# TensorE signals twice instead of four times per group: octet counts and early sums are waited for through the signal of the projected rows

## The chip, the cores and the metric

The kernel runs on one core of one Trainium2 chip. The time is the device time of one execution in microseconds (us). The kernel before takes 3303.69 us (median of 3 runs, 3300.82 to 3312.31). Differences of about 0.3% are the least that such runs tell from no change.

## The reference

Two graph layers over 12,500 nodes of 64 features and 212,500 edges sorted by destination (padded here to 208 groups of 1024 edges, 8 edges on each of 128 partitions):

```python
def _L0_gnn_ref(x, i, j, rbf, Wf1, bf1, Wf2, bf2, Wl, bl, gamma, beta):
    Wxh = x @ Wl.T + bl
    h = jax.nn.silu(rbf @ Wf1.T + bf1)
    f_ij = h @ Wf2.T + bf2
    msg = f_ij * Wxh[j]
    agg = jax.ops.segment_sum(msg, i, num_segments=x.shape[0])
    y = x + agg
    ...
def _L1_gnn_ref(x, edge_index, edge_weight, W1, b1, W2, b2):
    msg = x[src] * edge_weight[:, None]
    agg = jax.ops.segment_sum(msg, dst, num_segments=x.shape[0])
    h = jax.nn.relu((agg + x) @ W1 + b1)
    return h @ W2 + b2
...
edge_index = jnp.stack([src, dst])
x = _layernorm(x + _L0_gnn_ref(x, src, dst, edge_attr_64, edge_weight, ...), axis=-1)
x = _layernorm(x + _L1_gnn_ref(x, edge_index, edge_weight, ...), axis=-1)
```

The call is `_L0_gnn_ref(x, src, dst, edge_attr_64, ...)`: the first layer gathers at `dst` (sorted, so a group of edges needs only a short window of node rows) and sums at `src` (unsorted).

## The kernel before, in words

The change lies in `sorted_messages`, the first large stage. It walks over the 208 groups in 52 passes of S = 4 groups. For each group it computes the messages of 1024 edges, splits them into three bf16 parts, finds for each edge its rank within the block of 128 nodes it is summed into, and writes each edge's row to that block's region in memory (`region_rows`). There are 98 blocks. From pass 27 on the finished first rows of a block are already summed ("early sums"), one block per group, while later messages are still written: 7 tiles of 128 rows per block at first, 9 from pass 33, 10 from pass 39, 12 from pass 45 (`EARLY`), so groups 108, 132, 156 and 180 open these parts, and group 207 is the last.

Each engine has its own queue in program order, and engines meet only through semaphores. Per group (i, j), with the line numbers of the kernel before:

- TensorE (PE): `blocks` makes running counts by block from one-hot matrices (L1096, L1099, into `counts`) and the octet counts (L1102, L1104, into `ps_pairs`), and signals `rk` at L1104. `nodes` projects the node rows of the window onto the edges, six matmuls into `ps_x` (L1114), and signals `xw`. Then the two filter matmuls of the following groups (L1121, L1091), `back` (four transposes of the product, L1128), and `early_sums` (three matmuls a tile, L1138, signal `e_mm`).
- VectorE (DVE), in `steady`: `early_total` (L1252, adds an early sum to x), `products` (L1228), the one-hots and the window of the next group (L1179, L1181, L1188), `rest_part` (L1233), `earlier` of the next group (L1194 to L1199, where L1197 writes into a row buffer and first waits until the scatter of four groups before has landed, `sc[j]`), `low_part` (L1237, completes the rows of this group), `positions` of the next group (L1204 to L1221, where L1208 reads `counts`), and `early_onehot` (L1244).
- ScalarE (ACT): activations and the copies of the parts (L1026, L1030, L1035, L1039, L1049, L1051).
- GpSimd (POOL): `scatter`, eight indirect DMAs per group (their issue is L1332). A group's scatter waits for its positions (L1221) and for its last part (`lw`, signalled by L1237, which is the later one).
- SyncE (SP): loads of edge features, node windows and the finished rows of blocks (L974, L984, L986, L989).

`count_of(i, j, back)` is the number of groups done up to group (i, j), less `back`; each semaphore is seeded with S. After the last group, POOL waits for all scatters and the stage that sums the remaining rows begins (L1527 and on).

Of the kernel before, what the change touches and what calls it, by code (L numbers as in the profile page):

```python
# [78 lines left out]
def program(nc, n_nodes, n_edges, x, x_t, src, dst, dst_next, dst_rows, firsts, group_dst, ew, rbf, w, out, wxh_rows, x1_rows, sorted_rows, q_block_row,  # L79
# [13 lines left out]
    with ctx:  # L93
# [183 lines left out]
        def count_of(i, j, back=0):  # L277


            return i * S + (S + 1 + j - back)  # L280
# [579 lines left out]
        def sorted_messages():  # L860
# [31 lines left out]
            e_ld = [own(f"e_ld_{u}") for u in range(RING)]  # L892
            e_kc, e_oh, e_mm = (own(f"e_{k}") for k in ("kc", "oh", "mm"))
            at = width + T * D
# [52 lines left out]
            with nc.Block(no_gpsimd_drain=True) as block:  # L947
# [18 lines left out]
                def _(e):  # L966
                    r = rbf.rearrange("(b p) n -> b p n", p=P)
                    q = rel_rows.rearrange("(b t) p -> b (t p)", t=BATCH * T)
                    def early_load(n):
                        if n.opens:  # L970
                            for j in range(S):
                                e.wait_ge(sc[j], (early_starts[n.stage] - BEHIND) * (16 * T) + 16 * T)
                        e.wait_ge(e_mm, n.number + 1)
                        e.dma_start(early_rows[n.slot][:, 0:n.tiles * RW // 2],  # L974
                                    region_rows[bass.ds(n.number * STRIDE, n.tiles * P), :].rearrange("(p t) w -> p (t w)", p=P)
                                    ).then_inc(e_ld[n.slot], 16)
# [106 lines left out]
                def _(e):  # L1083
                    seed(e, rk, xw, bk, e_mm)
                    empty = block_iota[:, :, :].rearrange("p n t -> p (n t)")[:, 0:PAIRS]
# [7 lines left out]
                    def blocks(i, j):  # L1093
                        e.wait_ge(ww, count_of(i, j, 1))
                        for t in range(0, T, TQ):
                            e.matmul(counts, not_tri[:, :], onehot_n((j + 1) % 2)[:, :, t:t + TQ], start=(t == 0), stop=False)  # L1096
                        e.wait_ge(oh, count_of(i, j))
                        for t in range(0, T, TQ):
                            e.matmul(counts, tri[:, :], onehot_n(j % 2)[:, :, t:t + TQ], start=False, stop=(t + TQ == T))  # L1099
                        e.wait_ge(ob, count_of(i, j))  # L1100
                        for t in range(0, T, TQ):
                            e.matmul(ps_pairs[0:NB, 0:NB * TQ], block_of_octet[j % 2][:, 0, :], onehot_n(j % 2)[:, :, t:t + TQ],  # L1102
                                     start=False, stop=False)
                        last = e.matmul(ps_pairs[0:NB, NB * TQ:PAIRS], block_of_octet[j % 2][:, 1, :], moved[:, tiles(i, j)],  # L1104
                                        start=False, stop=False)
                        last.then_inc(rk, 1)

# [23 lines left out]
                    def early_sums(i, j, n):  # L1131
                        e.wait_ge(e_oh, n.number + 1)
                        e.wait_ge(m, count_of(i, j))
                        rows = early_rows[n.slot].bitcast(BF16).rearrange("p (t w) -> p t w", w=RW)
                        place = early_places[n.slot % 2][:, 0:P * n.tiles].rearrange("p (n t) -> p n t", t=n.tiles)
                        for t in range(n.tiles):
                            for c in range(PARTS):
                                last = e.matmul(early_sum, place[:, :, t], rows[:, t, c * D:(c + 1) * D],  # L1138
                                                start=(t == 0 and c == 0), stop=(t == n.tiles - 1 and c == PARTS - 1))
                        last.then_inc(e_mm, 1)  # L1140

# [31 lines left out]
                def _(e):  # L1173
                    seed(e, oh, ob, wi, c1, c2, c3, bs, ba, ww, pr, pr2, po, m, r1, lw, me)

                    def block_onehot(i, j):
                        e.wait_ge(rk, count_of(i, j, 1))
                        e.wait_ge(ww, count_of(i, j, 2))
# [22 lines left out]
                    def positions(i, j):  # L1201
# [3 lines left out]
                        e.wait_ge(ww, count_of(i, j, 1))  # L1205
                        e.wait_ge(rk, count_of(i, j))
                        e.wait_ge(ba, count_of(i, j, 1))
# [32 lines left out]
                    def early_onehot(n):  # L1240
                        e.wait_ge(e_kc, n.number + 1)
                        e.wait_ge(e_mm, n.number + S - 1)
                        place = early_places[n.slot % 2][:, 0:P * n.tiles].rearrange("p (n t) -> p n t", t=n.tiles)
                        e.tensor_tensor(place, early_keys[:, 0:1, bass.ds(n.at, n.tiles)].broadcast_to([P, P, n.tiles]),  # L1244
                                        iota_rep[:, :, 0:n.tiles], ALU.is_equal).then_inc(e_oh, 1)

                    def early_total(n):
                        e.wait_ge(e_mm, n.number + S + 1)
                        if isinstance(n.number, int) and n.number == 0:
# [5 lines left out]
                    def steady(i, j, now=None, before=None):  # L1255
                        if before and before.exists:
                            early_total(before)
                        products(i, j)
# [40 lines left out]
                    for j in range(S - 1):  # L1299
                        steady(passes - 1, j, unit(passes - 1, j, K, False), unit(passes - 1, j, K, False, 2))  # L1300
                    early_total(unit(passes - 1, S - 1, K, False, 2))
                    products(passes - 1, S - 1)
                    rest_part(passes - 1, S - 1)
                    low_part(passes - 1, S - 1)

                    e.wait_ge(rk, S * passes + S + 1)
                    step(e.tensor_reduce(run[:, :], counts.rearrange("p (n t) -> p n t", t=TQ), AX.X, ALU.add))
# [1267 lines left out]
```

## Time and profile before

| | |
|---|---|
| median of 3 runs | 3303.69 us |
| the profiled execution, its own time | 3301.68 us |
| its span in the profile | 3299.7 us |
| mean granted TensorE clock | 0.80 of full |
| busy share of the span | DVE 78%, POOL 71%, PE 62%, ACT 30% |
| message stage: first and last indirect DMA start on POOL | 129.7 us, 2258.9 us |

A busy share is an average over stages with different limits, so what bounds the message stage is read from that stretch alone. A duration is the time an engine held an instruction; "idle" is the time the engine stood before it, with what released it ("issue" where the profile names no releaser). The granted clock of TensorE is in tenths of its full 2.4 GHz; in the message stage it moves between its two levels, 1.0 (2.4 GHz) and 0.5 (1.2 GHz).

### The profile page before, as it was taken

What the parts mean: (1) busy time and instruction counts of PE and PEld (TensorE: products, weight loads), DVE (VectorE), ACT (ScalarE), POOL (GpSimd) and SP (SyncE); (2) the same over time, 40 slices, a digit from 0 to 9 for tenths busy, and PEclk for the clock granted to TensorE, in tenths of its full rate; (3) what the DMA queues carried; (4) which work ended last, traced back from release to release, by engine and by line L of the source; (5) the groups of instructions that cost most, each with busy time, mean ns of one, the idle gap of its engine ahead of it and who ended that gap; (6) DMA issues with size and microseconds to landing.
All of it is one profiled execution on the core that took longest, in us unless ns stands there. A gap on an engine that the chain in (4) does not pass through costs nothing. (4 is left out here: it accounts for less than half of the span.)

```text
span 3299.7 us, 57203 instructions
## 1 busy us (share of the span) xinstructions
PE 2051.3 (62%) x18002; PEld 1373.3 (42%) x18002; DVE 2563.1 (78%) x4987; ACT 1001.9 (30%) x2288; POOL 2335.0 (71%) x2177
## 2 busy tenths in 40 slices
PE   2655565656555556666676666663783666658886
PEld 2222222222222233333444444443773655547775
DVE  6877777777777777778787787774875999978887
ACT  3222222222222222222222222221676666641001
POOL 0677777777777777777777777774234888868775
PEclk8888878787887788888888888886755677769999
DMA  7743445333333334444444445434654999989997
GB/s 199 196 124 124 124 124 150 95 95 94 94 95 93 95 116 127 127 135 138 134 142 144 143 151 153 147 98 139 194 166 152 354 363 358 357 324 405 395 392 286
DMA packets 261217, 605.85 MB, mean 184 GB/s; under 512 B 112847, under 2 KB 130127, under 8 KB 248375
## 3 DMA queue, kind: packets, MB, share of 16 engines
q1 hardware_dynamic: 186330, 385.45, 38.1%
q0 software_dynamic: 67488, 210.15, 17.3%
q10 hardware_dynamic: 7205, 7.74, 0.9%
q8 instruction: 113, 1.85, 0.2%
q14 instruction: 81, 0.66, 0.1%
HBM read 403.92 MB, written 199.25 MB: 183 GB/s over the span
## 5 line engine op out<-in xcount | busy, mean ns | idle before, releaser
L1332 POOL DMA_INDIRECT region_rows<-x_space,pos x1664 | 1657.4, 996 | 531.4 <-issue 504.2
L1128 PE MATMUL ps_cnt<-ident,work 128*128 128x128 f32 x832 | 178.2, 353 | 760.2 <-DVE work L1228 760.2
L1035 ACT CAST x_space<-ps_cnt 128x512 bf16<-128x512 f32 x208 | 121.7, 585 | 1461.9 <-PE ps_cnt L1128 1461.9
L1128 PEld LDWEIGHTS ps_cnt<-ident,work 128*128 128x128 f32 x832 | 116.6, 176 | 931.2 <-issue 931.2
L1217 DVE TENSOR_REDUCE rank<-work 128x8 f32<-128x784 f32 x208 | 323.4, 1555 | 21.8 <-DVE work L1213 0.5
L1121 PE MATMUL ps_fx<-work,w_wf 128*128 128x512 f32 x416 | 253.6, 694 | 67.6 <-ACT work L1026 66.7
L1233 DVE TENSOR_TENSOR work<-ps_cnt,x_space 128x512 f32<-128x512 f32 x208 | 143.8, 691 | 124.8 <-ACT x_space L1035 124.8
L1091 PE MATMUL ps_th<-x_space,w_wf 128*128 128x512 f32 x416 | 220.4, 613 | 9.4 <-DMA x_space<-rbf 9.4
L1114 PE MATMUL ps_fx<-work,x_space 128*64 128x512 bf16 x1248 | 225.3, 478 | 0.0
L1213 DVE TENSOR_TENSOR work<-onehot,ps_rank 128x784 f32<-128x784 bf16 x208 | 201.9, 971 | 7.2
L1197 DVE COPY x_space<-edges_space 128x16 f32 (+1 forms) x208 | 39.8, 191 | 212.5 <-DMA region_rows<-x_space,pos 212.0
L2051 DVE TENSOR_TENSOR x_space<-x_space,iota_rep 128x3328 bf16<-128x3328 bf16 x98 | 195.9, 1999 | 3.6 <-PE ps_th L2090 0.2
L1871 PE MATMUL ps_th<-x_space,tmp_space 128*128 128x64 bf16 x1764 | 127.9, 222 | 102.8 <-DVE tmp_space L1834 102.8
L1039 ACT CAST x_space<-work 128x512 bf16<-128x512 f32 x208 | 128.6, 618 | 174.3 <-DVE work L1233 174.3
L1871 PE MATMUL ps_fx<-x_space,tmp_space 128*128 128x64 bf16 x1764 | 128.0, 222 | 72.1 <-DVE tmp_space L1834 72.1
L1834 DVE TENSOR_SCALAR tmp_space<-tmp_space,scalars 128x1152 bf16<-128x1152 bf16 x196 | 161.4, 824 | 10.5 <-DMA tmp_space<-key_rows 10.5
L1237 DVE TENSOR_TENSOR x_space<-work,x_space 128x512 bf16<-128x512 f32 x208 | 143.3, 689 | 31.8 <-ACT x_space L1039 30.7
L1908 POOL TENSOR_TENSOR x_space<-tmp_space,x_space 128x576 f32<-128x576 f32 x80 | 137.8, 1723 | 37.0 <-ACT x_space L1887 37.0
L1871 PEld LDWEIGHTS ps_th<-x_space,tmp_space 128*128 128x128 bf16 x1764 | 114.1, 116 | 116.5 <-DVE tmp_space L1834 116.5
L1096 PE MATMUL ps_rank<-onehot,not_tri 128*128 128x392 bf16 x416 | 156.2, 471 | 0.0
L1208 DVE TENSOR_REDUCE run<-ps_rank 128x98 f32<-128x392 f32 x208 | 116.3, 559 | 48.2 <-issue 43.8
L1099 PE MATMUL ps_rank<-onehot,tri 128*128 128x392 bf16 x416 | 152.0, 459 | 0.0
(276 smaller groups left out, 5322.1 us busy)
## 6 DMA issues: line engine op xcount, KB each, us to landing
tmp_space<-key_rows SPq DMA_DIRECT2D x98, 576.0 KB, 7.7
x_space<-rbf SPq DMA_DIRECT2D x104, 512.0 KB, 3.8
tmp_space<-rel_rows SPq DMA_DIRECT2D x104, 512.0 KB, 4.1
region_rows<-x_space,pos POOLq DMA_INDIRECT x1664
tmp_space<-region_rows SPq DMA_DIRECT2D x48, 441.0 KB, 4.1
tmp_space<-region_rows SPq DMA_DIRECT2D x25, 588.0 KB, 5.1
region_rows<-x_space SPq DMA_DIRECT2D x12, 1176.0 KB, 7.2
tmp_space<-region_rows SPq DMA_DIRECT2D x25, 539.0 KB, 4.5
```

Of the source, the lines that this page charges most:

```text
L1091: return e.matmul(ps_hid[j % 2], wts["wf1"][:, :], inputs_t[j], start=True, stop=True)
L1096: e.matmul(counts, not_tri[:, :], onehot_n((j + 1) % 2)[:, :, t:t + TQ], start=(t == 0), stop=False)
L1099: e.matmul(counts, tri[:, :], onehot_n(j % 2)[:, :, t:t + TQ], start=False, stop=(t + TQ == T))
L1114: last = e.matmul(ps_x[h * D:(h + 1) * D, :], near[j][:, c * D:(c + 1) * D], window_half(j, h), start=(c == 0), stop=(c == PARTS - 1))
L1121: return e.matmul(ps_f[:, :], wts["wf2"][:, :], hid[j % 2][:, :], start=True, stop=True)
L1128: last = e.transpose(ps_cnt[:, t * P:(t + 1) * P], product[:, t * P:(t + 1) * P], ident[:, :])
L1213: e.tensor_tensor(masked_n, onehot_n(j % 2), base_ps.unsqueeze(2).broadcast_to([P, NB, T]), ALU.mult).then_inc(ww, 1)
L1217: e.tensor_reduce(rank8[:, :], masked_n.rearrange("p n t -> p t n"), AX.X, ALU.add).then_inc(pr, 1)
L1332: e.indirect_dma_start(out=region_rows, out_offset=bass.IndirectOffsetOnAxis(ap=pos[j][:, t:t + 1], axis=0), in_=rows_f[j][:, t, :], in_of ...
L1834: e.tensor_scalar(which[n % 2], key_bc[b % KB][:, (n % 2) * U * P:(n % 2 + 1) * U * P], node_1, None, ALU.is_equal).then_inc(oh, 1)
L1871: last = e.matmul(ps_rows[n % 2][:, t, :], which[n % 2][:, t * P:(t + 1) * P], x1_part(n // 2, c), start=(c == 0), stop=(c == PARTS - 1))
L2051: e.tensor_tensor(places[c % 2], place[c % 2].unsqueeze(1).broadcast_to([P, P, RUN]), iota_rep[:, :, :], ALU.is_equal).then_inc(oh, 1)
```

## The change

The signals of `blocks` (`rk`, one a group) and of `early_sums` (`e_mm`, one a block) are taken away. Who waited for them waits for `xw`, which PE signals at the end of `nodes`, or for nothing where an earlier wait on `xw` on the same queue already covers it. `rk` is kept for the one last matmul after the loop. No matmul, DMA or vector instruction is added, removed or moved.

```diff
-                        e.wait_ge(e_mm, n.number + 1)
                         e.dma_start(early_rows[n.slot][:, 0:n.tiles * RW // 2],
...
-                    seed(e, rk, xw, bk, e_mm)
+                    seed(e, xw, bk)
...
-                        last = e.matmul(ps_pairs[0:NB, NB * TQ:PAIRS], block_of_octet[j % 2][:, 1, :], moved[:, tiles(i, j)],
-                                        start=False, stop=False)
-                        last.then_inc(rk, 1)
+                        e.matmul(ps_pairs[0:NB, NB * TQ:PAIRS], block_of_octet[j % 2][:, 1, :], moved[:, tiles(i, j)],
+                                 start=False, stop=False)
...
-                                last = e.matmul(early_sum, place[:, :, t], rows[:, t, c * D:(c + 1) * D],
-                                                start=(t == 0 and c == 0), stop=(t == n.tiles - 1 and c == PARTS - 1))
-                        last.then_inc(e_mm, 1)
+                                e.matmul(early_sum, place[:, :, t], rows[:, t, c * D:(c + 1) * D],
+                                         start=(t == 0 and c == 0), stop=(t == n.tiles - 1 and c == PARTS - 1))
...
                     def block_onehot(i, j):
-                        e.wait_ge(rk, count_of(i, j, 1))
+                        e.wait_ge(xw, count_of(i, j, 1))
...
                         e.wait_ge(ww, count_of(i, j, 1))
-                        e.wait_ge(rk, count_of(i, j))
+                        e.wait_ge(xw, count_of(i, j))
                         e.wait_ge(ba, count_of(i, j, 1))
                         e.tensor_reduce(run[:, :], counts.rearrange("p (n t) -> p n t", t=TQ), AX.X, ALU.add).then_inc(bs, 1)
...
                     def early_onehot(n):
                         e.wait_ge(e_kc, n.number + 1)
-                        e.wait_ge(e_mm, n.number + S - 1)
...
-                    def early_total(n):
-                        e.wait_ge(e_mm, n.number + S + 1)
+                    def early_total(n, i, j):
+                        e.wait_ge(xw, count_of(i, j))
...
-                    e.wait_ge(rk, S * passes + S + 1)
+                    e.wait_ge(rk, 1)
```

Below is VectorE's queue in a pass with early sums of 10 tiles, from the end of one group's positions to the product of the next group, before the change. In brackets stand the semaphores that an instruction waits for: stage0_15 is `rk`, stage0_12 is `xw`, stage0_40 is `e_mm`, stage0_38 is `e_kc`, stage0_20 is `ww`.

```order
L1204 TENSOR_REDUCE same<-same 128x8 [waits stage0_17,stage0_23]
L1208 TENSOR_REDUCE run<-ps_rank 128x98 [waits stage0_31,stage0_15,stage0_20]
L1211 TENSOR_TENSOR ps_rank<-ps_rank,run 128x98 [waits stage0_19,stage0_21]
L1221 SCALAR_TENSOR_TENSOR pos<-rank,edges_space 128x8 [waits stage0_22]
L1244 TENSOR_TENSOR x_space<-tmp_space,iota_rep 128x1280 [waits stage0_40,stage0_38]
L1252 TENSOR_TENSOR agg<-ps_agg,x_space 128x64 [waits stage0_40]
L1228 TENSOR_TENSOR work<-ps_fx,work 128x512 [waits stage0_12,stage0_10,stage0_11]
```

And the same place after it, where the lines have moved up by three or four:

```order
L1201 TENSOR_REDUCE same<-same 128x8 [waits stage0_17,stage0_23]
L1205 TENSOR_REDUCE run<-ps_rank 128x98 [waits stage0_31,stage0_12,stage0_20]
L1208 TENSOR_TENSOR ps_rank<-ps_rank,run 128x98 [waits stage0_19,stage0_21]
L1218 SCALAR_TENSOR_TENSOR pos<-rank,edges_space 128x8 [waits stage0_22]
L1240 TENSOR_TENSOR x_space<-tmp_space,iota_rep 128x1280 [waits stage0_38]
L1248 TENSOR_TENSOR agg<-ps_agg,x_space 128x64 [waits stage0_12]
L1225 TENSOR_TENSOR work<-ps_fx,work 128x512 [waits stage0_12,stage0_10,stage0_11]
```

The instructions stand in the same order; the reduction of the counts now waits for `xw` instead of `rk`, the early one-hot has one wait less, and the early total waits for `xw`.

## Rows read from the trace of the kernel before

**Rows 1.** The page, part 1: busy us, share of the span, instructions.
```profile
PE 2051.3 (62%) x18002; PEld 1373.3 (42%) x18002; DVE 2563.1 (78%) x4987; ACT 1001.9 (30%) x2288; POOL 2335.0 (71%) x2177
```

**Rows 2.** Busy by stretch: width, busy (instructions) per engine, PEclk, DMA share, GB/s.
```profile
130.00:1186.00 1056.00, 597.69 (x2163) 275.90 (x2162) 758.18 (x1654) 243.73 (x412) 807.41 (x816) 0.81 0.37 110
1433.00:1683.00 250.00, 168.61 (x1140) 99.23 (x1140) 199.70 (x436) 62.05 (x144) 191.47 (x193) 0.82 0.46 137
1683.00:1933.00 250.00, 169.77 (x1218) 103.33 (x1218) 200.16 (x438) 62.22 (x144) 191.16 (x194) 0.83 0.48 143
1933.00:2226.50 293.50, 199.71 (x1563) 127.78 (x1563) 232.85 (x500) 72.13 (x165) 225.69 (x223) 0.82 0.45 135
```

**Rows 3.** L1332, 130 to 2260 us: durations ns min/median/max, starts; idle by releaser.
```profile
L1332 POOL DMA_INDIRECT region_rows<-x_space,pos x1638: 965/969/1590, 129.7 to 2258.9; - x182
  issue: 496.9, 1630
```

**Rows 4.** L1197 in four stretches: durations, starts; then idle before it (us, times).
```profile
L1197 DVE COPY x_space<-edges_space x103: 167/176/372, 136.5 to 1184.8; 128x16 f32 x103
  DMA region_rows<-x_space,pos: 168.3, 62
...
L1197 DVE COPY x_space<-edges_space x24: 166/170/310, 1437.1 to 1676.3; 128x16 f32 x20, 128x16 f32<-128x16 f32 x4
  DMA region_rows<-x_space,pos: 9.9, 9
...
L1197 DVE COPY x_space<-edges_space x24: 166/170/377, 1686.6 to 1926.4; 128x16 f32 x20, 128x16 f32<-128x16 f32 x4
  DMA region_rows<-x_space,pos: 6.6, 4
...
L1197 DVE COPY x_space<-edges_space x28: 167/169/346, 1936.6 to 2224.2; 128x16 f32 x21, 128x16 f32<-128x16 f32 x7
```

**Rows 5.** Timeline at 2001 us, clock at its full level: start, us, instruction.
```profile
2000.87 0.17 PE L1104 MATMUL ps_agg<-edges_space,block_of_octet 128*98 x1
2000.96 0.84 PE L1114 MATMUL ps_fx<-work,x_space 128*64 128x512 bf16 x6
2001.13 0.57 DVE L1208 TENSOR_REDUCE run<-ps_rank 128x98 f32<-128x392 f32 x1 [0.37 <-issue]
```

**Rows 6.** Timeline at 1438 us, clock at its lower level.
```profile
1438.49 0.21 PE L1104 MATMUL ps_agg<-edges_space,block_of_octet 128*98 128x8 bf16 x1
1438.62 1.50 PE L1114 MATMUL ps_fx<-work,x_space 128*64 128x512 bf16 x6
```

**Rows 7.** L1208 in the last three stretches: durations, starts; idle before it.
```profile
L1208 DVE TENSOR_REDUCE run<-ps_rank x24: 554/566/568, 1438.8 to 1678.6; 128x98 f32<-128x392 f32 x24
  issue: 10.2, 17
...
L1208 DVE TENSOR_REDUCE run<-ps_rank x24: 548/567/568, 1688.8 to 1928.6; 128x98 f32<-128x392 f32 x24
  issue: 10.5, 21
...
L1208 DVE TENSOR_REDUCE run<-ps_rank x28: 565/567/568, 1938.8 to 2225.7; 128x98 f32<-128x392 f32 x28
  issue: 21.9, 27
```

**Rows 8.** L1114 on PE, stretches from 1433 and from 1933: durations, starts.
```profile
L1114 PE MATMUL ps_fx<-work,x_space x144: 378/403/636, 1438.6 to 1679.2; 128*64 128x512 bf16 x144
...
L1114 PE MATMUL ps_fx<-work,x_space x168: 378/379/637, 1938.7 to 2226.0; 128*64 128x512 bf16 x168
```

**Rows 9.** Timeline at the stage's end: last L1237, first DMA of group 207, next stage.
```profile
2234.13 0.69 DVE L1237 TENSOR_TENSOR x_space<-work,x_space 128x512 bf16<-128x512 f32 x1 [0.68 <-ACT x_space L1039]
...
2249.98 0.96 POOL L1332 DMA_INDIRECT region_rows<-x_space,pos  x1 [0.30 <-issue]
...
2262.26 1.28 ACT L1527 ACT_TABLE_LOAD   x1 [28.16 <-PEq L947]
```

More of the change, by code:

```diff
@@ L892, in sorted_messages @@
             e_ld = [own(f"e_ld_{u}") for u in range(RING)]
-            e_kc, e_oh, e_mm = (own(f"e_{k}") for k in ("kc", "oh", "mm"))
+            e_kc, e_oh = (own(f"e_{k}") for k in ("kc", "oh"))
             at = width + T * D
@@ L1256, in steady @@
                         if before and before.exists:
-                            early_total(before)
+                            early_total(before, i, j)
                         products(i, j)
@@ L1300, in _ @@
                         steady(passes - 1, j, unit(passes - 1, j, K, False), unit(passes - 1, j, K, False, 2))
-                    early_total(unit(passes - 1, S - 1, K, False, 2))
+                    early_total(unit(passes - 1, S - 1, K, False, 2), passes - 1, S - 1)
                     products(passes - 1, S - 1)
```

## The prediction

> **What bounds the kernel now.** I first read the page's busy shares. They name VectorE (78%) ahead of GpSimd (71%) [rows 1], which is an average over all stages. The change acts only in the message stage, so I read that stage alone. Its indirect DMAs start from 129.7 to 2258.9 us, and 1630 of the 1638 waited for nothing but their own issue: 496.9 / 1630 = 0.30 us each, behind 0.97 us of work [rows 3]. GpSimd is therefore a solid chain of 1.27 us steps, eight a group, a little over 10.2 us a group (191.47 us busy in 250 is the same 0.97 in 1.27) [rows 2]. It is never starved after the start. The message stage ends when GpSimd ends, and the next stage starts 2 to 3 us later [rows 9].
>
> VectorE runs ahead of GpSimd. How far, and with what slack, decides this change. Two readings give it:
>
> - The brake. L1197 may not fill a row buffer before the scatter of four groups ago has landed. Where VectorE stands there, it has time to spare. Up to 1186 us it stood 168.3 us in 103 groups, 1.6 us a group. From 1433 it stood 9.9 us in 24 groups, from 1683 6.6 us in 24, and from 1933 not at all in 28 [rows 4]. So VectorE, which also does early one-hots and totals there, has spare time at first and none at the end.
> - The lead. For the last group, L1237 ends at 2234.13 + 0.69 = 2234.82, and GpSimd starts that group's scatter at 2249.98 [rows 9]. The rows lie finished for 15.2 us. This is the stock that can be eaten before GpSimd waits.
>
> Then I looked at what VectorE waits for in the late part. L1208, which reads the running counts, stood 10.2, 10.5 and 21.9 us in the last three stretches, before 17 of 24, 21 of 24 and 27 of 28 groups [rows 7]. The profile calls this "issue", but the timeline shows whose it is: at 2001 us the octet matmul L1104 ends at 2000.87 + 0.17 = 2001.04 and L1208 starts at 2001.13, after 0.37 us idle [rows 5]. It is the wait on `rk`. So in the late part VectorE is bound through TensorE: early sums, then the counts, then L1208.
>
> **The change, part by part.**
>
> *L1208 waits for `xw` instead of `rk`.* It now starts after the six matmuls of L1114 too, which stand right behind L1104. At the full clock they end at 2000.96 + 0.84 = 2001.80, 0.76 us behind L1104 [rows 5]. At the lower clock they end at 1438.62 + 1.50 = 1440.12, 1.42 us behind its 1438.70 [rows 6]. In a group where L1208 already waited, all of this is added. The instructions behind it on VectorE (positions, early one-hot, total, the next product) are late by as much, and so are the transposes and early sums on TensorE, which wait for that product, and ScalarE's copies. They all hang on VectorE's chain and shift with it, so nothing makes the time good except the stand at L1197.
>
> I moved the start of each L1208 to the end of that group's last L1114 plus the 0.09 us seen between L1104 and L1208. The added delay sums to 19.9 us in the 24 groups from 1433 (0.83 each), 20.1 us in the next 24 (0.84) and 22.3 us in the last 28 (0.80). These means lie near the full-clock 0.76, as they should: the median L1114 takes 379 to 403 ns, the longest 636 [rows 8], so most groups see the full clock and some the lower. Sum: 62.3 us.
>
> *What is absorbed.* Before 1433 all of it: the delay is under 1.5 us in any group, adds to 34.6 us over 131 groups, and the stand at L1197 is many times that (168.3 us up to 1186 alone) [rows 4]. From 1433, following the groups in order and letting each stand at L1197 swallow the lateness collected so far, 8.0 of the 9.9 us are used, and 6.3 of the 6.6. VectorE then is late by 62.3 - 8.0 - 6.3 = 48.0 us at the last group.
>
> *What is left on the end.* The lead of 15.2 us covers the first part; it is used up near group 170 (about 1835 us), and from there GpSimd waits once a group for L1237. 48.0 - 15.2 = 32.8 us remain. The stages behind start when the last scatter is done, so they shift by this whole.
>
> *The other waits.* `block_onehot` waits for `xw` of a group whose product has just waited for the same count: nothing. `early_total` waits for `xw` of the group whose product stands right behind it, and that count has been waited for already in the positions before: nothing new. `early_onehot` and SyncE's loads of block rows lose a wait that an earlier `xw` wait covers. The transfers are issued when the queue comes to them, as before. What a dropped wait frees on VectorE no row shows. I bound it by the 0.09 us from the end of L1104 to the start of L1208 [rows 5], over 76 groups 7 us, and from below by 0; I take 0, since the remaining wait of the same instruction stays.
>
> *Taking the signals off TensorE.* The octet matmul with its signal ends at 2001.04, and L1114 has started at 2000.96, before it [rows 5]. The signal holds nothing up, so I take 0. The most it could hide is the 0.09 us between the starts of the two matmuls (2000.87 and 2000.96); for two signals over 76 groups that is 14 us, which I keep for the range. The Trainium skill, "TensorE: Matmul & The Clock Gate", section "The cost: per-tile semaphore tail", says that increments on completion serialize at about 26 ns each; it speaks for this change. By it, two signals less in each of 76 groups would give back an estimated 4 us, and the sum would be 29 instead of 33. The trace does not show such a tail behind L1104.
>
> *The sum.* The profiled execution took 3301.7 us, and 3301.7 + 32.8 = 3334.5. The median of the runs lies 2.0 us above that execution, so I forecast 3336, 1.0% slower. Bounds of this mechanism: with the 7 us of the dropped wait and the 14 us of the signals it is 33 - 21 = 12 (3316); another 0.09 us a group, should `xw` come through later than `rk`, gives 33 + 7 = 40 (3344).
>
> **The rivals.**
>
> - *The lead swallows it: no change.* VectorE works 15 us ahead and stands at L1197 for 16.5 us from 1433 on [rows 4, 9], so up to 15.2 + 14.3 = 29.5 us over 76 groups cost nothing. This decides when the real delay is under 29.5 / 76 = 0.39 us a group, half of what the rows show. It could be so if the modelled ends of matmuls stood too late, or if VectorE came to L1208 later for another reason. The start of L1208 0.09 us behind the modelled end of L1104 [rows 5] speaks against it. Time: 3304. Chance 0.12.
> - *Faster: collisions ease.* GpSimd's issue takes 965 ns at best but up to 1590 [rows 3], perhaps where it meets VectorE's wide operations; the mean up to 1186 us is 807.41 / 816 = 989 ns [rows 2]. If VectorE's shifted position took such meetings away, the gain is at most 0.024 us x 1638 = 39 us. It decides only if GpSimd stays the bound, so the lead has to hold as well, and VectorE still runs as many wide operations per group. A third of it gives 3304 - 13 = 3291. Chance 0.03.
> - *Slower still: TensorE's clock.* TensorE now idles 0.8 us longer in each late group. The granted clock is 0.82 to 0.83 there [rows 2]. If it fell to the lower level throughout, L1114 would add 1.42 instead of 0.82 a group, another 46 us over 76, besides longer early sums. A part of this, 15 to 30 us, gives 3350 to 3366. Against it: up to 1186 us TensorE is busy for only 57% of the time, and its clock is 0.81 all the same, as against 68% and 0.82 at the end [rows 2]. So I give it 0.10.
> - The mechanism as summed: 0.75.
>
> **How the numbers follow.** The likeliest case alone gives 3316 to 3344. For 8 in 10 I reach down into the lead rival (partly absorbed) and up to the lower end of the clock rival: 3311 to 3351. A measurement here tells about 0.3% (10 us) from no change. Faster: 0.03. Same: the lead rival, 0.12. Slower: 0.85.
>
> **What would show it.** In the profile after: the idle before the counts' reduction (now L1205) rises from 21.9 us to about 44 in the last 28 groups. GpSimd waits for L1234 (was L1237) at about one DMA in eight from some 1840 us on, some 33 us in all. The stand at L1194 (was L1197) in the stretches from 1433 nearly vanishes. The stretch up to 1186 and all after the message stage keep their length. The prediction is wrong if GpSimd is still never starved at 2200 us, if the reduction starts before the last L1112 (was L1114) ends, or if the added time lies behind the message stage.

## The result and the profile after

The changed kernel takes 3369.72 us (median of 4 runs, 3366.35 to 3373.26), the kernel before on the same chip 3302.26 us. The ratio is 1.020, interval 1.0175 to 1.0221: slower by 67 us, where 33 us were forecast, and outside the stated range (3311 to 3351).

The page of the changed kernel, part 1, in the columns of [rows 1]. VectorE, ScalarE and GpSimd are busy for at most 6 us more. TensorE is busy for 37.2 us more with the same 18002 matmuls, 15 us of it before 1189 us, where nothing is lost (next table). The span is longer by 68.7 us.

```profile
span 3368.4 us, 57021 instructions
...
PE 2088.5 (62%) x18002; PEld 1397.5 (41%) x18002; DVE 2569.0 (76%) x4987; ACT 1001.9 (30%) x2288; POOL 2338.0 (69%) x2177
```

Busy time by stretch, as in [rows 2]: the first is the same stretch without early sums, the others are groups 132 to 155, 156 to 179 and 180 to 207.

```profile
133.00:1189.00 1056.00, 612.74 (x2165) 283.26 (x2163) 760.85 (x1655) 243.63 (x413) 807.84 (x815) 0.81 0.37 110
1440.00:1711.00 271.00, 171.42 (x1142) 101.93 (x1143) 201.71 (x439) 62.06 (x144) 205.94 (x204) 0.80 0.44 129
1711.00:1985.00 274.00, 173.97 (x1228) 106.06 (x1227) 201.35 (x439) 62.28 (x145) 191.65 (x193) 0.80 0.44 131
1985.00:2308.50 323.50, 208.25 (x1557) 131.01 (x1555) 230.93 (x495) 72.05 (x165) 226.36 (x220) 0.79 0.40 121
```

Up to 1189 us GpSimd issues 815 DMAs where it issued 816: nothing is lost there. The three stretches of early sums take 271, 274 and 324 us where they took 250, 250 and 294, and their granted clock is 0.80, 0.80, 0.79 instead of 0.82, 0.83, 0.82.

The counts' reduction (now L1205) in the same stretches, as in [rows 7]:

```profile
L1205 DVE TENSOR_REDUCE run<-ps_rank x24: 565/567/568, 1445.3 to 1704.7; 128x98 f32<-128x392 f32 x24
  issue: 34.1, 24
...
L1205 DVE TENSOR_REDUCE run<-ps_rank x24: 565/567/567, 1716.8 to 1977.9; 128x98 f32<-128x392 f32 x24
  issue: 36.6, 24
...
L1205 DVE TENSOR_REDUCE run<-ps_rank x28: 565/566/567, 1990.1 to 2307.0; 128x98 f32<-128x392 f32 x28
  issue: 51.7, 28
```

It now stands in every group, for 34.1, 36.6 and 51.7 us against 10.2, 10.5 and 21.9. The period is (1704.7 - 1445.3) / 23 = 11.28 us a group, then 11.35 and 11.74, against 10.43, 10.43 and 10.63. The stand at the row buffer (now L1194) has no row in any of the three.

A group of the last stretch in the timeline: the reduction starts 0.11 us behind the end of L1112 (2011.28 + 0.84 = 2012.12), not behind L1103, and GpSimd waits for the last part of the rows.

```profile
2010.20 0.69 DVE L1234 TENSOR_TENSOR x_space<-work,x_space 128x512 bf16<-128x512 f32 x1 [0.29 <-ACT x_space L1038]
...
2011.18 0.17 PE L1103 MATMUL ps_agg<-edges_space,block_of_octet 128*98 128x8 bf16 x1
...
2011.28 0.84 PE L1112 MATMUL ps_fx<-work,x_space 128*64 128x512 bf16 x6
...
2011.74 0.97 POOL L1328 DMA_INDIRECT region_rows<-x_space,pos  x1 [0.79 <-DVE x_space L1234]
...
2012.23 0.57 DVE L1205 TENSOR_REDUCE run<-ps_rank 128x98 f32<-128x392 f32 x1 [1.21 <-issue]
```

GpSimd over the whole stage, as in [rows 3]. It is starved 79 times, in the last third of the stage; the first time that it stands for more than 1 us is in group 153. (These waits include the 0.30 us that each issue costs anyway.)

```profile
L1328 POOL DMA_INDIRECT region_rows<-x_space,pos x1639: 963/969/1728, 130.1 to 2327.2; - x183
  issue: 487.3, 1560
  DVE x_space L1234: 61.8, 53
  DVE pos L1218: 7.9, 26
```

The end of the stage, as in [rows 9]: the last L1234 ends at 2315.83, and the first DMA of the last group starts at 2318.25. The lead has shrunk from 15.2 to 2.4 us. By the same reading, group by group, it is under 1.5 us for the first time in group 150, where the prediction had it used up near group 170.

```profile
2315.14 0.69 DVE L1234 TENSOR_TENSOR x_space<-work,x_space 128x512 bf16<-128x512 f32 x1 [0.68 <-ACT x_space L1038]
...
2318.25 0.97 POOL L1328 DMA_INDIRECT region_rows<-x_space,pos  x1 [0.30 <-issue]
...
2330.54 1.28 ACT L1523 ACT_TABLE_LOAD   x1 [15.44 <-PEq L947]
```

The balance closes. The last reduction of counts starts at 2307.0 instead of 2225.7, 81.3 us later; the lead gives back 15.2 - 2.4 = 12.8; and the last group's scatter starts 2318.25 - 2249.98 = 68.3 us later. The next stage begins 2330.54 - 2262.26 = 68.3 us later, and nothing is added behind it.

So place and chain are as forecast, and the loss is twice the forecast one. **Where the other half of the loss lies.** At group 107, before any early sum, the changed kernel's execution is already 3.1 us later. That leaves 78.2 us of lateness made in groups 108 to 207, where the prediction had 48.0. Going through the trace of before once more, row by row, with another rule for the stands at L1197 gives 64.5 (theory B below; 63.5 with the 0.09 us of the prediction between the rows' end and the reduction, 65.4 with the 0.11 us seen after). Some 3.3 us of it arise in groups 108 to 131, where the prediction had nothing; the reductions of groups 107 and 131 lie 3.2 us farther apart after than before.

That leaves 13.7 us. TensorE's way can be measured by itself: from the start of the product to the end of the projected rows took 5.94, 5.99 and 6.14 us on average in the three stretches before, and takes 6.03, 6.13 and 6.49 after; 24 x 0.09 + 24 x 0.14 + 28 x 0.35 = 15 us, with the granted clock down as above. The same sum is 17 us for e2 below, which has the same wait moved, and 3.5 us for e1, which is as fast as the kernel before, so it holds to a few us.

**Theory A** is the prediction's: lateness is swallowed by each stand at the row buffer. **Theory B**: the stand lies behind the product in VectorE's queue, and TensorE's way (transposes, early sums, counts, rows) starts at the product. The two run side by side. Where TensorE's way is the longer one, arriving late at the stand shortens only the shorter way, and nothing is given back. A stand gives back at most the time by which VectorE's own way is longer. B was made up after the result; the runs below test it.

### The profile page after: what moved, and what is told of

It is laid out like the page before. It is cut to its first block and busy times, and to the rows that moved or that the text cites. A ratio compares the mean times of both kernels' runs of the same rounds, so it can differ in the third digit from the quotient of the medians.

```text
span 3368.4 us, 57021 instructions
## 1 busy us (share of the span) xinstructions
PE 2088.5 (62%) x18002; PEld 1397.5 (41%) x18002; DVE 2569.0 (76%) x4987; ACT 1001.9 (30%) x2288; POOL 2338.0 (69%) x2177
## 3 DMA queue, kind: packets, MB, share of 16 engines
q1 hardware_dynamic: 186330, 385.45, 37.2%
## 5 line engine op out<-in xcount | busy, mean ns | idle before, releaser
L1126 PE MATMUL ps_cnt<-ident,work 128*128 128x128 f32 x832 | 191.6, 374 | 824.9 <-DVE work L1225 824.9
L1126 PEld LDWEIGHTS ps_cnt<-ident,work 128*128 128x128 f32 x832 | 124.8, 187 | 994.8 <-issue 994.8
L1205 DVE TENSOR_REDUCE run<-ps_rank 128x98 f32<-128x392 f32 x208 | 117.0, 562 | 160.1 <-issue 155.2
L1112 PE MATMUL ps_fx<-work,x_space 128*64 128x512 bf16 x1248 | 232.2, 490 | 0.0
L1234 DVE TENSOR_TENSOR x_space<-work,x_space 128x512 bf16<-128x512 f32 x208 | 143.4, 689 | 38.0 <-ACT x_space L1038 37.3
L1904 POOL TENSOR_TENSOR x_space<-tmp_space,x_space 128x576 f32<-128x576 f32 x80 | 138.0, 1725 | 37.2 <-ACT x_space L1883 37.2
L1194 DVE COPY x_space<-edges_space 128x16 f32 (+1 forms) x208 | 40.0, 192 | 158.8 <-DMA region_rows<-x_space,pos 158.5
```

The costliest lines, as they stand in the source:

```text
L1112: last = e.matmul(ps_x[h * D:(h + 1) * D, :], near[j][:, c * D:(c + 1) * D], window_half(j, h), start=(c == 0), stop=(c == PARTS - 1))
L1126: last = e.transpose(ps_cnt[:, t * P:(t + 1) * P], product[:, t * P:(t + 1) * P], ident[:, :])
```

## The experiments

**Which wait, and do signals cost?** The first gives the changed kernel its signal at the octet counts back; the second moves only one wait in the kernel before.

```diff
 # e1, against the changed kernel
-                        e.matmul(ps_pairs[0:NB, NB * TQ:PAIRS], block_of_octet[j % 2][:, 1, :], moved[:, tiles(i, j)],
+                        last = e.matmul(ps_pairs[0:NB, NB * TQ:PAIRS], block_of_octet[j % 2][:, 1, :], moved[:, tiles(i, j)],
...
+                        last.then_inc(rk, 1)
...
                     def positions(i, j):
-                        e.wait_ge(xw, count_of(i, j))
+                        e.wait_ge(rk, count_of(i, j))
...
 # e2, against the kernel before
                     def positions(i, j):
-                        e.wait_ge(rk, count_of(i, j))
+                        e.wait_ge(xw, count_of(i, j))
```

> The changed kernel with one signal given back: the octet matmul signals again, and only the reduction of the counts waits for it; the signal of the early sums stays away and every other wait stays on the projected rows. If the whole loss is the wait of the counts' reduction (theory A and B alike), this is the kernel before: 3302 us, ratio to before 0.998 to 1.002. If a part of the loss comes from the early totals, the early one-hots or SyncE's loads, now ordered through the projected rows, this part stays: with half of the loss 3335 us.

> The kernel before with one wait moved: the reduction of the counts waits for the projected rows; all four signals are still given and all other waits are as before. If the loss is that wait: 3370 us, ratio 1.020, within 5 us of the changed kernel. If signals on TensorE cost what the Trainium skill's figure gives (an estimated 4 to 5 us for two signals in each of some 76 to 98 groups), it is that much above the changed kernel, 3375. If the other waits carried a part, it is below 3360.

Measured: e1 3297.4 us against 3296.5, ratio 1.0007 (0.9994 to 1.0019). e2 3367.4 us, ratio 1.0225 (1.0199 to 1.0251). The one wait of the counts' reduction is the whole loss. The early totals, the one-hots and SyncE's loads on another signal are worth nothing (e1, to within 6 us). For the signals taken off TensorE the times are too coarse to settle 4 us: e2 gives them all and is as slow as the changed kernel, but each of the two ratios is known to some 8 us only. The traces settle it. In the groups from 108 on whose six row matmuls ran at 2.4 GHz, the first of them starts 97 ns (median) behind the start of the octet matmul, in the kernel before, in e1 and in e2, where that matmul signals, and in the changed kernel, where it does not. From the start of the last early sum to that of the next counts matmul the medians are 59 ns before, 60 in e2 and 59 after. A signal holds up nothing here. GpSimd's waits in e2:

```profile
L1332 POOL DMA_INDIRECT region_rows<-x_space,pos x1637: 963/969/1735, 130.0 to 2327.4; - x182
  issue: 490.9, 1571
  DVE x_space L1237: 55.8, 45
  DVE pos L1221: 6.4, 21
```

**The dose.** The changed kernel with two, or eight, instead of six matmuls ahead of the signal.

```diff
                     def nodes(i, j):
 # e3
-                            for c in range(PARTS):
-                                last = e.matmul(ps_x[h * D:(h + 1) * D, :], near[j][:, c * D:(c + 1) * D],
-                                                window_half(j, h), start=(c == 0), stop=(c == PARTS - 1))
+                            last = e.matmul(ps_x[h * D:(h + 1) * D, :], near[j][:, 0:D],
+                                            window_half(j, h), start=True, stop=True)
...
 # e4
-                            for c in range(PARTS):
+                            for n_, c in enumerate((0, 0, 1, 2)):
...
```

> The changed kernel with a smaller dose: the node rows are projected from the first of their three bf16 parts alone, so two matmuls stand between the octet counts and the signal instead of six, and the second and third part are left out of the result. The added delay per group falls from about 0.8 to about 0.3 us. Theory A, the bookkeeping of the prediction (each stand at the row buffer swallows the lateness collected so far): lateness at the last group 16 us, 2 us of it beyond the lead, time 3304. Theory B (a stand swallows nothing in a group where the way over TensorE is the longer one, since that way starts at the product, ahead of the stand): lateness 25 us, 11 us beyond the lead, time 3313.

> The changed kernel with a larger dose: the first part is added twice, eight matmuls instead of six ahead of the signal, so the projected rows are not those of the reference. Theory A: 50 us beyond the lead, time 3352. Theory B: 74 us beyond the lead from the row by row account alone, and with the 14 to 17 us that the changed kernel showed beyond that account (a longer way over TensorE at a lower granted clock, some us of the start) 3390 us.

Measured: e3 3309.4 us, ratio 1.0042 (1.0026 to 1.0057), 13 us over the kernel before; A had 2, B 11. e4 3391.0 us, ratio 1.0294 (1.0268 to 1.0320), 94 us; A had 50 (64 to 67 if it is given the 14 to 17 us of TensorE's longer way too), B 88 to 91 with them. The lateness made in groups 108 to 207, by the starts of the reduction in the traces, is 20 us in e3 (A 16, B 25) and 108 in e4 (A 65, B 89, both without TensorE's longer way, which from the product to the end of the octet counts alone is 14 us longer in e4 than before). The larger dose rules A out even with that share: 65 + 14 = 79 against 108. The smaller one does not decide: its time speaks for B, its lateness lies midway, and its profiled execution, at 3298.3 us, was the fastest of eight, 11 us under their median. No stand at the row buffer is left in groups 132 to 207 of either.

**TensorE's clock.** The changed kernel with 30 small matmuls a group more, in the gap ahead of the transposes.

```diff
                         if left > 2:
                             after(hidden, i, j, 2)
+                        for _ in range(30):
+                            e.matmul(ps_pairs[0:NB, PAIRS:512], tri[:, 0:NB], not_tri[:, 0:512 - PAIRS], start=False, stop=False)
                         back(i, j)
...
```

> The changed kernel with 30 small matmuls (112 columns each) more per group on TensorE, in the gap in which it waits for the product, into columns that nothing reads. If the way over TensorE is longer in the changed kernel because the longer gap costs granted clock, the share of the lower level falls, the last stretch's period goes from 11.75 to about 11.3 us a group, and the time is 3350 to 3356. If the granted clock has nothing to do with the gap, 3370. If the filling itself is too long for the gap (at the lower clock it may be), the transposes start late and the time is over 3375.

Measured: 3340.2 us, ratio 1.0117 (1.0091 to 1.0144), faster than the expectation had even for the case that the clock is the cause. By the ratios, useless matmuls take back (1.0198 - 1.0117) x 3302 = 27 us of the 67. From 1433 to 2250 us the profiles give, for the kernel before:

```profile
1433.00:2250.00 817.00, 540.15 (x3928) 331.54 (x3928) 639.48 (x1387) 197.60 (x455) 626.14 (x627) 0.82 0.45 135
```

for the changed kernel:

```profile
1433.00:2250.00 817.00, 521.86 (x3671) 318.36 (x3670) 596.77 (x1293) 186.19 (x431) 589.19 (x582) 0.80 0.44 132
```

and with the gap filled:

```profile
1433.00:2250.00 817.00, 618.36 (x6006) 431.56 (x6004) 618.24 (x1328) 191.05 (x443) 613.00 (x601) 0.87 0.45 135
```

The granted clock is the last but two: 0.82, 0.80, 0.87. With the wait moved, TensorE idles longer in each group and is granted less; kept busy in the idle time, it is granted more than in the kernel before. Time at the 1.2 GHz level from group 132 to 207 is 35%, 41% and 26%. From product to rows takes 5.68, 5.68 and 6.16 us in the three stretches with the gap filled, 28 us less in sum than in the changed kernel and 13 less than in the kernel before. So the 27 us gained lie on TensorE's way, and they are more than the 14 to 15 us of the change, since the fill also takes back some of what the lower level costs in the kernel before. The Trainium skill, "TensorE: Matmul & The Clock Gate", in its section "Why this matters for your kernels", advises against idle gaps between bursts of matmuls; the traces of this kernel on these chips agree.

The gap itself is TensorE's idle time ahead of the transposes, which wait for the product. One tile's instructions on PE, durations and starts, then the idle time before them, first in the changed kernel, then in the kernel before:

```profile
L1126 PE MATMUL ps_cnt<-ident,work x304: 272/421/448, 1440.8 to 2302.0; 128*128 128x128 f32 x152
...
  DVE work L1225: 316.1, 76
```

```profile
L1128 PE MATMUL ps_cnt<-ident,work x304: 272/303/448, 1434.5 to 2222.3; 128*128 128x128 f32 x152
...
  DVE work L1228: 259.0, 76
```

It is 316.1 / 76 = 4.2 us a group after and 259.0 / 76 = 3.4 before, and the median transpose takes 421 ns instead of 303.

**Early sums into the gap.** The sums moved ahead of the transposes (`early_sums` before `back`), the total behind `low_part` of the same group with a signal for TensorE.

> The changed kernel with two signals kept, but the early sums moved from behind the transposes to ahead of them, into the gap in which TensorE waits for the product; the early total moves on VectorE to behind the last part of the same group, one group sooner, and signals TensorE. The 2.3 us of sums leave the way from the product to the counts. Theory B: that way falls from 6.5 to about 4.2 us, VectorE's own work becomes the longer way (period under 10.2 us if it were free), the stands at the row buffer come back, GpSimd is never starved, time 3302 (ratio 0.998 to 1.003). If the moved wait on the projected rows costs by itself, wherever TensorE's work lies, it stays slower than 3330.

Measured: 3335.8 us, ratio 1.0094 (1.0078 to 1.0109). B missed it (3302). By its number the run falls to the other side of the expectation (over 3330), but not by its mechanism: the moved wait hardly acts here. The reduction of the counts stood for 5.1 us in all before 14 of 76 groups:

```profile
L1205 DVE TENSOR_REDUCE run<-ps_rank x76: 550/556/568, 1441.6 to 2273.2; 128x98 f32<-128x392 f32 x76
  issue: 5.1, 14
```

The timeline shows that the sums are not in the gap:

```profile
2104.80 0.96 DVE L1240 TENSOR_TENSOR x_space<-tmp_space,iota_rep 128x1536 bf16<-128x1536 bf16 x1 [0.20 <-issue]
2105.68 0.68 DVE L1225 TENSOR_TENSOR work<-ps_fx,work 128x512 f32<-128x512 f32 x1
2105.89 2.40 PE L1136 MATMUL ps_agg<-tmp_space,x_space 128*128 128x64 bf16 x36 [3.10 <-DVE x_space L1240]
...
2108.11 1.09 PE L1126 MATMUL ps_cnt<-ident,work 128*128 128x128 f32 x4
```

They wait for the early one-hot (L1240), which VectorE writes last before the product (L1225). So they begin only as the gap ends, and the transposes, which ScalarE and VectorE wait for, start 2.43 us behind the product here and 2.03 on average, against 0.83 in the kernel before and in the changed one. VectorE stands 149.4 us in 77 groups for ScalarE's copy of the transposed product, against 43.9 in 76 before. So the sums, started this late, hold up VectorE's way instead. e6 says nothing on whether the moved wait can be hidden.

**Where in the group does a delay count?** One vector operation more per group in the kernel before (half of the ranks' product, into a buffer that is overwritten), ahead of the counts' reduction (e7) or behind it (e8).

```diff
+                        e.tensor_tensor(masked_n[:, 0:NB // 2, :], onehot_n(j % 2)[:, 0:NB // 2, :],
+                                        block_iota[:, 0:NB // 2, :], ALU.mult).then_inc(xt, 1)
```

> The kernel before with one vector operation of about 0.5 us more per group, placed ahead of the reduction of the counts, that is beside TensorE's way from the product to the counts. Theory B: it is hidden behind that way where TensorE is the longer one and swallowed by the stands elsewhere; row by row it leaves 3 us of lateness at the last group and nothing beyond the lead: 3302, ratio 0.999 to 1.002. If any 0.5 us in VectorE's group counted in the late part, 76 x 0.5 = 38 us less the stands and the lead: 3310 to 3320.

> The kernel before with the same vector operation just behind the reduction of the counts, in series with TensorE's way. Theory B: it counts in full where TensorE is the longer way and the stands give nothing back there: lateness 33 us, 18 us beyond the lead, time 3320 (ratio 1.004 to 1.007), and some us more if the granted clock falls as in the changed kernel. By the bookkeeping of the prediction (38 us less 14 us of stands less 15 us of lead) 3311.

Measured: e7 3317.5 us, ratio 1.0036 (1.0022 to 1.0050); e8 3313.6 us, ratio 1.0031 (1.0020 to 1.0042). The times don't tell the theories apart: GpSimd is hardly starved in either. This is e7:

```profile
L1337 POOL DMA_INDIRECT region_rows<-x_space,pos x1641: 965/969/1725, 129.3 to 2279.8; - x183
  issue: 497.8, 1633
  DVE x_space L1242: 1.8, 6
```

The leads do say something: 16.4 us at the last group in e7 and 7.5 in e8 (15.2 before). From group 131 to 207 VectorE falls back by 8.0 us in e7, in step with GpSimd, and by 16.3 in e8. Ahead of the reduction the 0.56 us mostly hid; behind it they ate half of the lead. There they lengthened the stretch from reduction to product by only 0.26 us on average, since they partly filled a semaphore gap, which is why e8 was smaller than planned. Of 76 x 0.26 = 20 us, 16 are left at the end, though L1197 had 16.5 us of stands to give: that fits B better than A. The time lost in both came from elsewhere, for which the last section has a partial answer.

**Runs that settle nothing.** On three other chips the kernel before took 4076, 4083 and 4086 us instead of 3300, so the runs made on them can't be set beside the others. The granted clock is 0.70 to 0.74 in them where it was 0.81 in the stretch up to 1186 us [rows 2]; this row is of e9:

```profile
133.00:1189.00 1056.00, 529.71 (x1714) 238.66 (x1715) 681.53 (x1481) 194.16 (x328) 656.08 (x654) 0.71 0.30 90
```

GpSimd is starved there from the first groups on, so the question of the stage's lead doesn't arise. The extra time lies in the message stage alone: from the last reduction of counts to the end takes 1054 us in e9 and 1074 in the kernel before. e9 and e10 are e7 and e8 with the other half of the operation as well, e11 is the kernel before with the fill of e5, and e12 is e6 with sums and totals a group later. e13 to e18 are the same kernels again.

> The kernel before with two vector operations of 0.56 us more per group, ahead of the reduction of the counts. The single one ahead cost 11 us without ever starving GpSimd, whose mean step went from 996 to 1006 ns. Twice that is some 20 us. Beside it theory B (hidden beside TensorE's way, up to its length) gives 24 to 28 us of lateness and 8 to 12 us beyond the lead: 3322 to 3335. If the place in the group did not matter, it is as slow as the kernel with the two behind the reduction.

> The same two operations just behind the reduction of the counts. The single one of 0.56 us lengthened the stretch from the reduction to the next product by only 0.27 us, since it fills a semaphore gap; the second one counts in full, so 0.84 us a group in series. Theory B: lateness 60 us, 44 us beyond the lead, and with GpSimd's slower steps up to group 131 (some 12 us) 3350 to 3362. By the bookkeeping of the prediction 76 x 0.84 less 14 less 15 = 34, and 12: 3340 to 3348, and if the place did not matter the same as with the two ahead.

> The kernel before with the 30 small matmuls per group in TensorE's gap. The share of time at the lower clock falls as it did in the changed kernel (0.41 to 0.26 from group 132 on), but GpSimd is the bound all through the stage: 3302, ratio 0.998 to 1.002, with a larger lead at the last group (over 17 us instead of 15). If TensorE's clock bounds this kernel anywhere in the stage, it is faster by 5 us or more.

> The kernel with the sums in the gap, mended: in it the sums waited for the early one-hot, which VectorE writes last before the product, so they started only as the gap ended (the sums waited 3.1 to 3.4 us for L1240 in a group) and the transposes came behind them. Here the sums and the total of a block come one group later, when its one-hot has long been written, so they can fill the gap; SyncE's loads wait for the total instead. Still two signals from TensorE per group beside the transposes' and those of the filters. Theory B: the way from product to counts falls from 6.5 to about 4.2 us, stands at the row buffer come back, GpSimd is never starved: 3302, ratio 0.998 to 1.003. If the later signal costs whatever TensorE's order is, over 3330.

> The kernel with two vector operations ahead of the reduction of the counts, where the kernel before takes its usual 3300 us. Expected as for its first run: 3322 to 3335 by theory B.

> The kernel with two vector operations behind the reduction of the counts. Expected as for its first run: 3350 to 3362 by theory B, 3340 to 3348 by the prediction's bookkeeping, and as with the two ahead if the place did not matter. The lateness at the last group in the trace tells it more finely: 60 us by theory B, 50 by the bookkeeping (64 less 14).

> The kernel before with the 30 small matmuls per group in TensorE's gap: 3302, ratio 0.998 to 1.002, the lead at the last group over 17 us, the share of the lower clock from group 132 on near 0.26.

> The kernel with two signals in which sums and totals come one group later, in TensorE's gap: 3302, ratio 0.998 to 1.003, GpSimd never starved. If the later signal costs whatever TensorE's order is, over 3330.

> Two vector operations behind the reduction of the counts, where the kernel before takes some 3300 us: 3350 to 3362 by theory B (60 us of lateness at the last group), 3340 to 3348 by the prediction's bookkeeping (50 us). Where the kernel before again takes over 4000 us, nothing of either.

> Two signals, sums and totals one group later in TensorE's gap: ratio 0.998 to 1.003 where the kernel before takes some 3300 us, GpSimd never starved; over 1.009 if the later signal costs whatever TensorE's order is.

Measured, as ratios to the kernel before on the same chip: two operations ahead 1.0080 and 1.0064, two behind 0.9752, 0.9781 and 0.9767, gap filled 1.0371 and 1.0367, sums later 0.9724, 0.9716 and 0.9696 (intervals of 0.004 to 0.010 to either side). They repeat well, but they tell of a kernel whose limit is elsewhere. There the filled gap made it slower and work behind the counts made it faster, where B has no change and a loss for the usual limit. What sets that limit was not found. Whether the sums a group later would hide the moved wait at 3300 us stays open.

## Why the prediction was wrong

- *The wait moves from L1104 to the last of six L1114, and L1208 starts late by 0.8 us in the late groups:* right. The start 0.11 us behind the rows' end shows it, and e1 and e2 show that this wait is all of the loss.
- *GpSimd is the chain that ends the stage, VectorE's lead covers the first part and is used up near group 170:* right in kind. The lead was gone 20 groups sooner, near group 150; at the last group 12.8 of the 15.2 us were used, and the stages behind shifted by the whole of the rest.
- *"Letting each stand at L1197 swallow the lateness collected so far, 8.0 of the 9.9 us are used, and 6.3 of the 6.6":* this step failed. (So did *"Before 1433 all of it"*, by some 3 us.) The stands lie beside TensorE's way and give nothing back where that way is the longer. In the trace of before, 13.2 of their 16.5 us stood in groups in which L1208 did not wait; once all 76 groups wait, none is left, and VectorE is not faster for it. Redone with that rule the account gives 64.5 us of lateness and 49 beyond the lead, instead of 48.0 and 33. The rule itself is inferred; e4 bears it out and rules the old one out (108 us of lateness, where A has 65, or 79 with TensorE's longer way). e3 was too small to, and e8 only leans its way.
- *TensorE's way stays as long as it was* (the sum has it at nothing): this failed too, by 14 to 15 us. That was the rival with the clock, put at 15 to 30 us and a chance of 0.10, as something that comes instead of the likeliest case. It came on top of it. The reason given against it was that TensorE's busy share and its clock do not go together in the trace of before. That is so after as well (busy for 58% at 0.81 up to 1189 us, 64% at 0.79 in the last stretch), but it said nothing on idle time inside a group. e5 shows that the gap and the clock belong together; that the whole 14 us are the clock's was not shown by itself.
- *The sum redone:* 64.5 + 13.7 + 3.1 (late before the early sums) - 12.8 (lead used) = 68.5 us, against 68.3 between the two profiled executions. The 13.7 are the remainder, so that this closes is no proof; with the 15 us measured on TensorE's way it is 70. The 3.1 us are not explained. The two executions differ by 2.1 us already at the first scatter, so most of them lie ahead of the groups.
- *Signals and dropped waits are worth 0:* right (e1, e2 and the 97 ns in both traces). The Trainium skill, "TensorE: Matmul & The Clock Gate", section "The cost: per-tile semaphore tail", from which the prediction estimated 4 us, speaks of many increments by matmuls on several tiles at a time; for one increment at the end of a burst the traces show no such tail.
- *The idle before the reduction rises from 21.9 to about 44 in the last 28 groups:* 51.7. It holds the stands that vanished from the queue ahead of it and the longer way over TensorE.

## What to carry to other kernels

A signal that rides on a later instruction costs the time between the two wherever its waiter was already standing; ask that first, for a signal by itself held nothing up here. When you follow a delay through a trace, an idle time gives it back only if it lies in series with the delay: draw both ways from the point at which they part to the point at which they meet, and take the longer. And a longer idle gap on TensorE may be paid a second time, in the granted clock of the work behind it.

## What the hardware showed unexpectedly

- Filling TensorE's idle gap with useless matmuls made the changed kernel some 27 us faster, at a granted clock of 0.87 instead of 0.80 from 1433 to 2250 us. On the chips on which the kernel before took 4080 us the same fill made that kernel 3.7% slower.
- One more vector operation of 0.56 us a group (two bf16 operands) may lengthen GpSimd's DMA issues. Over all 1664 issues their mean is 996 ns before, 1006 in e7 and 1003 in e8, but also 1005 in e2, which has no operation more. Up to group 107, before any early sum and before the loss sets in, the mean is 986 to 993 ns in the eight traces without the operation (before, changed, e1 to e6), 995 in e8 and 999 in e7. Against the 991 of the kernel before that is 7 us in e7 and 3.5 in e8 over the first 864 issues, a part of what the two kernels lost (11 and 7 us). That the two engines get in each other's way was not tried by itself, and the difference is little more than that between other traces.

The rows of the pages, part 5, with busy time and mean ns, of the kernel before, of e7 and of e2:

```profile
L1332 POOL DMA_INDIRECT region_rows<-x_space,pos x1664 | 1657.4, 996 | 531.4 <-issue 504.2
```

```profile
L1337 POOL DMA_INDIRECT region_rows<-x_space,pos x1664 | 1674.4, 1006 | 534.5 <-issue 503.9
```

```profile
L1332 POOL DMA_INDIRECT region_rows<-x_space,pos x1664 | 1673.0, 1005 | 583.7 <-issue 498.2
```
